# A 3x3 attention and convolution kernel: TensorE's loop over four image pairs is written out

## Chip, cores, metric

The kernel runs on one core of a Trainium2 chip. The metric is the device time of one launch in microseconds. TensorE (PE) does the matmuls, VectorE (DVE) and ScalarE (ACT) read its results from PSUM and prepare its next inputs, and SyncE (SP) issues nearly all DMAs. Each engine has its own program and its own loops; they meet only at semaphores.

## What is computed

```
x: [8,128,128,64] f32
q = x Q ; k, v = (3x3 neighbourhood of x) K, V
alpha = softmax over the 9 neighbours of (k . q) * mask
t_in = x + sum(alpha * v)
t = relu(conv3x3(t_in, ff1) + b1)      # 64 -> 64
t = relu(conv3x3(t,    ff2) + b2)      # 64 -> 128
t = relu(conv3x3(t,    ff3) + b3)      # 128 -> 64
out = t_in + t
```

## The kernel before

The eight images are worked as four pairs (`PAIRS`), two images side by side in the partitions. A pair is cut into 16 bands of 8 rows (`BANDS`) and takes 17 steps (`STEPS`, k = 0 to 16). A step runs the first and second convolution on one band, the third behind it, and the attention of the next band (at k = 16 that is the first band of the next pair); only step k = 15 (`BANDS - 1`) has no attention. The convolutions use a transformed form in which each row is split into four streams; the streams 2 and 1 are the "inner" ones and 0 and 3 the "outer" ones.

Every engine walks the same 17 steps for the four pairs. ACT, DVE and SP use `schedule` (L192 to L202): a hardware loop over the pairs (L193), in it steps 0 and 1, a hardware loop over steps 2 to 13 two at a time (L197), and steps 14, 15 and 16. TensorE has its own copy of this (L616 to L623): a hardware loop over the pairs (L616), steps 0 and 1, a hardware loop of 13 equal steps (L620), steps 15 and 16. Inside a hardware loop the counts to which a wait compares depend on the loop's registers, so each engine computes them with register instructions.

The order of work on TensorE at a step's start is what the prediction follows. `r_product(b)` (L372) makes the attention's first product in two PSUM banks, and `masks` (L388) presets the score banks. `conv1(..., outer=False)` (L445) does the inner streams of the first convolution. It may start when DVE has read the banks it overwrites (L871). With attention, it stops before the fourth of its first four weight sets (`await_r(b, 0)`, L464) until ACT has copied the result of `r_product` to SBUF (`keep_r`, L644, semaphore `r_ready`). Then come the rest of the inner streams, the scores of the first half (L396), and the outer streams (`outer=True`, also L445), for which DVE must have made the outer inputs (`t_inputs`, part 1, L799). The third convolution is L487, the second L503.

At a step's end `end2` (L503) does the last matmuls; its last two wait in `await_band` for DVE's additions (L781). In the last step of a pair (k = 16) DVE and ACT then still finish both halves of the second convolution (DVE L871, ACT L698, DVE L794 to L799) before they branch back to the top of their own pair loop.

Of the kernel before, what the change touches and what calls it, by code (L numbers as in the profile page):

```python
# [14 lines left out]
PAIRS = IMAGES // 2  # L15
# [59 lines left out]
def build(nc, x_bands, x_keys, qt2, kt, vbd, w1, w2, w3, b1, b2, b3, window, eye, eye16, out):  # L75
    with ExitStack() as ctx:
# [280 lines left out]
        def _(pe):  # L357
# [220 lines left out]
            def step(G, k, b, att):  # L578
                if att:
                    r_product(b)  # L580
                    masks()
                conv1(G, k, b, False, att)
                if att:
                    scores(b, 0)
                conv1(G, k, b, True)
                conv3_tile(G, k, 0)
                conv3_tile(G, k, 1, (lambda: await_prob(b, 0)) if att else None)
                if att:
                    turn(b, 0)
                conv3_tile(G, k, 2, (lambda: await_r(b, 1)) if att else None)  # L590
                if att:
                    masks()
                    scores(b, 1)
                conv3_tile(G, k, 3)
                if att:
                    mix(b, 0)
                begin2(G, k, 0)
                go_on2(G, k, 0)
                begin2(G, k, 1, (lambda: await_prob(b, 1)) if att else None)
                if att:  # L600
                    turn(b, 1)
                go_on2(G, k, 1)
                end2(G, k, 0)
                end2(G, k, 1)
                if att:
                    mix(b, 1)
                begin2(G, k, 2, (lambda: await_y(b)) if att else None)
                if att:
                    v_product(b)
                go_on2(G, k, 2)  # L610
                begin2(G, k, 3)
                go_on2(G, k, 3)
                end2(G, k, 2)
                end2(G, k, 3, lambda: await_band(b + 1 if att else b))

            with pe.Fori(0, PAIRS) as p:  # L616
                g0, b0 = p * STEPS, p * BANDS
                step(g0, 0, b0 + 1, True)
                step(g0 + 1, 1, b0 + 2, True)
                with pe.Fori(0, BANDS - 3) as h:  # L620
                    step(g0 + h + 2, 2, b0 + h + 3, True)
                step(g0 + (BANDS - 1), BANDS - 1, b0 + BANDS, False)
                step(g0 + BANDS, BANDS, b0 + BANDS, True)  # L623
# [433 lines left out]
```

## Time and profile before

| | us |
|---|---|
| median of 3 runs | 2279.57 (2278.01 to 2281.26) |
| the profiled execution | 2280.64 |
| its span, first to last instruction | 2278.5 |
| PE busy | 2183.9 (96%) |
| DVE busy | 1888.2 (83%) |
| ACT busy | 1132.8 (50%) |
| mean granted TensorE clock | 0.994 |

The profiled execution is 2.1 us longer than its span and 1.07 us above the median. In the views, times are us from the span's start. `PE` is a matmul and `PEld` a weight load; names that end in q (`PEldq`, `ACTq`, `DVEq`) are register and branch instructions of that engine's sequencer, which the busy time leaves out. The pairs begin on TensorE at about 49, 603, 1158 and 1713 us.

### The profile page before, as it was taken

How to read it: one execution, taken by the hardware profiler on the slowest of the kernel's cores; microseconds unless marked ns; L12 is line 12 of the kernel's file. 1: busy time of each engine (PE TensorE's matmuls, PEld its weight loads, DVE VectorE, ACT ScalarE, POOL GpSimd, SP SyncE). 2: the span in 40 equal slices, each digit the busy share in tenths (PEclk: the TensorE clock that was granted, in tenths of full speed). 3: DMA queues.
4: the chain of work that ended last, by engine and by line, in shares of the span. 5: the costliest groups of instructions: out<-in, count | busy, mean ns of one | idle time of the engine just before them, and what ended most of it. 6: DMA issues, size and time to landing. Idle time of an engine off the chain costs nothing.

```text
span 2278.5 us, 63905 instructions
## 1 busy us (share of the span) xinstructions
PE 2183.9 (96%) x24401; PEld 1226.9 (54%) x24401; DVE 1888.2 (83%) x2850; ACT 1132.8 (50%) x3108; POOL 15.5 (1%) x24
## 2 busy tenths in 40 slices
PE   4999999999899999999989999999988999999998
PEld 2655555555455555555455555555545555555554
DVE  4788888888688888888768888888877888888886
ACT  2555555544454554555345554555435555555543
POOL 2000000000000000000000000000000000000000
PEclk9999999999999999999999999999999999999999
DMA  5445544544355445544345455445434554454453
GB/s 131 137 138 154 157 146 133 166 151 135 98 164 160 147 132 163 153 145 132 128 139 154 132 168 148 144 137 168 145 122 116 169 146 142 142 167 144 139 152 124
DMA packets 291271, 328.54 MB, mean 144 GB/s; under 512 B 89300, under 2 KB 223252, under 8 KB 284564
## 3 DMA queue, kind: packets, MB, share of 16 engines
q1 hardware_dynamic: 291164, 327.17, 48.1%
q8 instruction: 60, 0.98, 0.2%
q14 instruction: 47, 0.39, 0.1%
HBM read 152.50 MB, written 33.82 MB: 82 GB/s over the span
## 4 chain that ended last, share of the span: by engine, by line
PE 86%; DVE 7%; issue 3%; ACT 2%; DMA 1%; SPq 1%; DVEq 0%; ACTq 0%
PE conv_banks L487 30%; PE conv_banks L503 24%; PE conv_banks L445 16%; PE mix_bank L423 5%; PE score_banks L396 4%; DVE work L871 3%; PE score_banks L408 3%; PE mix_bank L435 3%; PE score_banks L388 1%; DMA work<-w 1%; ACT probt L649 1%; DVE prob L770 0%; DVE negmax L761 0%; ACT relued L698 0%; PE mix_bank L372 0%
## 5 line engine op out<-in xcount | busy, mean ns | idle before, releaser
L487 PE MATMUL conv_banks<-dodd,w3f 128*64 128x512 f32 (+1 forms) x1656 | 500.8, 579 | 12.6 <-DVE work L838 9.8
L487 PE MATMUL conv_banks<-deven,w3f 128*64 128x512 f32 (+1 forms) x1656 | 494.7, 568 | 8.7 <-DVE prob L770 7.0
L632 ACT ACTIVATE prob<-score_banks,negmax 128x100 f32<-128x100 f32 x1040 | 343.0, 343 | 194.9 <-DVE negmax L761 194.9
L445 PE MATMUL conv_banks<-dt,w1f 128*64 128x256 f32 (+3 forms) x4224 | 413.4, 383 | 12.2 <-DVE work L871 5.6
L503 PE MATMUL conv_banks<-duh,w2h 64*128 64x512 f32 (+2 forms) x1632 | 327.7, 399 | 4.0 <-ACT m_sb L668 2.1
L445 PEld LDWEIGHTS conv_banks<-dt,w1f 128*64 128x64 f32 (+1 forms) x4224 | 219.0, 135 | 207.2 <-issue 71.2
L503 PE MATMUL conv_banks<-duh,w2l 64*128 64x512 f32 (+2 forms) x1632 | 318.7, 387 | 6.0 <-DVE prob L770 5.2
L503 PE MATMUL conv_banks<-dul,w2h 64*128 64x512 f32 (+2 forms) x1632 | 282.0, 396 | 0.9 <-DVE tf L781 0.9
L487 PEld LDWEIGHTS conv_banks<-dodd,w3f 128*64 128x64 f32 x1656 | 138.9, 137 | 237.6 <-issue 212.8
L649 ACT COPY probt<-score_banks 100x1024 f32<-100x1024 f32 x130 | 131.7, 1013 | 234.8 <-PE score_banks L408 234.8
L487 PEld LDWEIGHTS conv_banks<-deven,w3f 128*64 128x64 f32 x1656 | 155.8, 138 | 155.2 <-issue 111.5
L644 ACT COPY rq<-mix_bank 128x512 f32<-128x512 f32 x65 | 38.2, 587 | 387.2 <-PE mix_bank L372 387.2
L761 DVE TENSOR_REDUCE negmax<-score_banks 128x4 f32<-128x400 f32 x260 | 148.3, 571 | 98.5 <-PE score_banks L396 97.9
L632 ACT ACTIVATION_READ_ACCUMULATOR prob<-score_banks,negmax 128x1 f32 x1040 | 212.1, 204 | 0.0
L698 ACT ACTIVATE relued<-work,bias 128x1024 f32<-128x1024 f32 (+2 forms) x136 | 149.4, 1102 | 92.2 <-DVE work L871 92.2
L871 DVE TENSOR_TENSOR work<-conv_banks,work 128x1024 f32<-128x1024 f32 (+2 forms) x136 | 157.1, 1160 | 43.6 <-PE conv_banks L503 43.6
L503 PEld LDWEIGHTS conv_banks<-dul,w2h 64*128 64x128 f32 x1632 | 143.1, 185 | 75.5 <-issue 53.4
L503 PEld LDWEIGHTS conv_banks<-duh,w2l 64*128 64x128 f32 x1632 | 153.6, 185 | 49.4 <-ACT rq L639 15.2
L503 PEld LDWEIGHTS conv_banks<-duh,w2h 64*128 64x128 f32 x1632 | 153.2, 184 | 47.2 <-ACT m_sb L668 3.9
L668 ACT COPY m_sb<-conv_banks 128x512 f32<-128x512 f32 (+3 forms) x205 | 108.2, 562 | 137.0 <-PE conv_banks L487 98.5
L423 PEld LDWEIGHTS mix_bank<-probt,xk 100*64 100x64 f32 x4160 | 139.4, 139 | 58.0 <-issue 56.8
L811 DVE TENSOR_TENSOR dul<-work,duh 128x1024 fp32r<-128x1024 f32 (+1 forms) x136 | 159.0, 1169 | 0.0
(93 smaller groups left out, 2942.1 us busy)
## 6 DMA issues: line engine op xcount, KB each, us to landing
xk<-x_keys SPq DMA_DIRECT2D x66, 800.0 KB
xc<-x_bands SPq DMA_DIRECT2D x66, 650.0 KB, 5.0
dodd<-dodd SPq DMA_DIRECT2D x68, 512.0 KB, 5.1
xr<-x_bands SPq DMA_DIRECT2D x264, 128.0 KB, 3.4
out<-work SPq DMA_DIRECT2D x60, 512.0 KB, 2.7
dt<-dt SPq DMA_DIRECT2D x68, 256.0 KB, 2.3
deven<-deven SPq DMA_DIRECT2D x68, 256.0 KB, 5.6
duh<-duh SPq DMA_DIRECT2D x68, 256.0 KB, 2.4
```

The costliest lines, as they stand in the source:

```text
L396: mm = nc.tensor.matmul(banks[n][to, a], rq[rows, patch], xc[rows, :, patch * PATCH:patch * PATCH + HALO], start=False, stop=a == GROUP - 1)
L423: last = nc.tensor.matmul(mix_bank[image, a * C:(a + 1) * C], xk[:, patch, image], probt[:, half, i if a < GROUP else 1 - i, a], start=Tru ...
L445: mm = nc.tensor.matmul(bank[(LOWER, UPPER)[o], n * 256 + lo * 64:n * 256 + hi * 64], w1f[i][rows, m, s, o * C:o * C + C], dt[rows, lo + s ...
L487: return nc.tensor.matmul(bank[rows, lo * 128:hi * 128], w3f[:, m, s, odd * C:odd * C + C], source[:, lo + s // 2:hi + s // 2, m], start=s ...
L503: return nc.tensor.matmul(conv_banks[:, bank_of(which, j), lo * 128:hi * 128], w[rows, STREAMS[j], 2 * (which == EVEN) + s], d[rows, lo + ...
L632: last = nc.scalar.activation(prob[:, g % 2, a], score_banks[:, g % 2, a * KEYS:(a + 1) * KEYS], ACT.Exp, bias=negmax[:, g % 2, a:a + 1], ...
L649: nc.scalar.copy(probt[:, half], score_banks[0:KEYS].rearrange("n i (a q) -> n i a q", q=C)).then_inc(probt_ready, 1)
L668: nc.scalar.copy(m2_sb[:, which % 2, lo:hi], bank[:, lo:hi]).then_inc(act_read, 1)
L698: nc.scalar.activation(to[:, lo:hi, :, 1:1 + W], sums[which][:, lo:hi], ACT.Relu, bias=bias[:, 1:2]).then_inc(relu_done, 1)
L761: nc.vector.tensor_reduce(negmax[:, g % 2], score_banks[:, g % 2, 0:GROUP * KEYS].rearrange("q (a n) -> q a n", n=KEYS), AX_X, ALU.max, ne ...
L811: nc.vector.tensor_tensor(dul[:, 1:n + 1, streams], du[:, 0:n, streams], duh[:, 1:n + 1, streams].bitcast(F32), ALU.subtract).then_inc(du_ ...
L871: nc.vector.tensor_tensor(both, m03, both, ALU.add).then_inc(dve_read, 1)
```

## The change

TensorE's loop over the pairs becomes a loop of the program that builds the kernel, so the four bodies stand one behind the other in TensorE's program. `p`, `g0` and `b0` are then numbers. The loop over the 13 equal steps inside it stays a hardware loop, four times. The other engines are as before, with their loops over the pairs.

```
@@ -613,7 +613,7 @@
                 end2(G, k, 2)
                 end2(G, k, 3, lambda: await_band(b + 1 if att else b))
 
-            with pe.Fori(0, PAIRS) as p:
+            for p in range(PAIRS):
                 g0, b0 = p * STEPS, p * BANDS
                 step(g0, 0, b0 + 1, True)
                 step(g0 + 1, 1, b0 + 2, True)
```

## Rows read from the trace of the kernel before

**Rows 1.** The page, chain that ended last: shares of the span by engine
```profile
PE 86%; DVE 7%; issue 3%; ACT 2%; DMA 1%; SPq 1%; DVEq 0%; ACTq 0%
```

**Rows 2.** Who waited for whom, TensorE: us in total, times, longest
```profile
PE mix_bank L372 <- issue: 11.2, 3, 3.8
```

**Rows 3.** Line 616, TensorE's pair loop: ns min/median/max, first and last start
```profile
L616 PEldq COMPARE_BRANCH  x4: 83/3764/3870, 599.1 to 2263.9; - x4
```

**Rows 4.** Line 620, TensorE's inner loop, same columns
```profile
L620 PEldq COMPARE_BRANCH  x52: 76/215/247, 146.0 to 2205.9; - x52
```

**Rows 5.** Chain in order of time, an inner step: start us, us, what
```profile
1029.95 1.24 DVE work L871
...
1031.23 2.97 PE conv_banks L445 x32
```

**Rows 6.** Timeline around the first pair boundary: start, us, instruction, [idle before <- releaser]
```profile
599.01 0.33 PE L503 MATMUL conv_banks<-dul,w2h 64*128 64x128 f32 x2 [0.23 <-DVE tf L781]
...
600.12 0.74 DVE L871 TENSOR_TENSOR work<-conv_banks,work 128x256 f32<-128x256 f32 x2
...
601.28 0.51 ACT L698 ACTIVATE relued<-work,bias 128x256 f32<-128x256 f32 x1
...
602.97 1.12 PE L372 MATMUL mix_bank<-xc,qk 64*64 64x512 f32 x2 [3.64 <-issue]
...
604.99 0.58 ACT L644 COPY rq<-mix_bank 128x512 f32<-128x512 f32 x1 [3.21 <-PE mix_bank L372]
605.08 1.23 DVE L799 TENSOR_TENSOR dt<-tf 128x1024 f32<-128x1024 f32 x1 [1.77 <-issue]
...
605.22 6.00 PE L445 MATMUL conv_banks<-dt,w1f 128*64 128x256 f32 x31
...
612.01 5.54 PE L445 MATMUL conv_banks<-dt,w1f 128*64 128x256 f32 x32
```

**Rows 7.** Chain in order of time, the same boundary: conv1's two pieces
```profile
605.29 1.80 PE conv_banks L445 x12
...
607.20 3.96 PE conv_banks L445 x19
```

**Rows 8.** Line 193 at the three boundaries: ACT's branch, then its next instruction
```profile
L193 ACTq COMPARE_BRANCH  x1: 50/50/50, 601.0 to 601.0; - x1
L193 ACTq FUSED_REGOPS  x1: 73/73/73, 603.8 to 603.8; - x1
...
L193 ACTq FUSED_REGOPS  x1: 73/73/73, 1159.6 to 1159.6; - x1
...
L193 ACTq FUSED_REGOPS  x1: 73/73/73, 1714.4 to 1714.4; - x1
```

**Rows 9.** Timeline of TensorE at the second and third boundary
```profile
1167.67 0.65 PE L445 MATMUL conv_banks<-dt,w1f 128*64 128x256 f32 x4
...
1714.85 7.27 PE L445 MATMUL conv_banks<-dt,w1f 128*64 128x256 f32 x31
...
1722.90 1.30 PE L445 MATMUL conv_banks<-dt,w1f 128*64 128x256 f32 x10
```

**Rows 10.** Windows: stretch, its us, busy us (instructions) by engine, granted clock, DMA
```profile
602.57:605.98 3.41, 3.01 (x16) 1.08 (x18) 1.64 (x3) 0.99 (x2) 0.00 (x0) 0.50 0.70 178
...
1131.63:1135.05 3.42, 3.42 (x10) 1.00 (x8) 3.39 (x5) 1.31 (x8) 0.00 (x0) 0.50 0.02 5
...
1155.53:1162.35 6.82, 3.88 (x20) 1.56 (x22) 4.03 (x10) 2.29 (x5) 0.00 (x0) 0.50 0.60 141
...
1711.90:1718.72 6.82, 6.12 (x30) 2.73 (x30) 2.08 (x3) 1.07 (x2) 0.00 (x0) 0.50 0.65 174
```

**Rows 11.** Who waited for whom, TensorE, another wait of 2.2 us
```profile
PE conv_banks L487 <- DVE work L838: 9.8, 8, 2.2
```

**Rows 12.** Line 538, register instructions of TensorE: ns min/median/max
```profile
L538 PEldq ALU_OP  x204: 32/32/32, 75.7 to 2261.9; - x102
```

**Rows 13.** The page, DMA queues: packets, MB, share of 16 engines
```profile
q8 instruction: 60, 0.98, 0.2%
```

More of the change, by code:

```diff
@@ L614, in step @@
                 end2(G, k, 3, lambda: await_band(b + 1 if att else b))
-            with pe.Fori(0, PAIRS) as p:
+            for p in range(PAIRS):
                 g0, b0 = p * STEPS, p * BANDS
```

## The prediction

> **What bounds the kernel now.** I read the chain that ended last first: TensorE holds 86% of it [rows 1], so time comes off only where TensorE's own timeline gets shorter. Then I read who waited for whom. Among TensorE's waits stands one with the releaser "issue", that is, no semaphore: three times before L372, 11.2 us in total, 3.8 the longest [rows 2]. L372 is the first matmul of a step, and three is the number of returns to the top of the pair loop. The view of line 616 confirms it: the branch takes 3.70 to 3.87 us when taken (the minimum, 83 ns, is the last one, which falls through) [rows 3]. The branch of the inner loop takes 215 ns [rows 4], and in the inner step that I looked at it costs nothing: the convolution after it starts when DVE's L871 ends, and TensorE is then busy to the end of the step [rows 5]. So the change touches three stretches of some 10 us. The question for each is what is late next once the branch is gone.
>
> **What happens at a boundary.** In the first one, TensorE's last matmul ends at 599.01 + 0.33 = 599.34, the branch holds it until 602.97, and the second half of conv1 (the outer streams) begins at 612.01 [rows 6]. ACT and DVE keep their pair loops. ACT's branch starts at 601.0, its last work of the pair (L698) ends at 601.8, and its next instruction, a register operation, appears at 603.8 only, though it waits for nobody [rows 6, 8]. So ACT too pays about 2.8 us for going back. Today nobody sees that: the copy (L644) starts at 604.99, released by TensorE's L372, because TensorE was later still. DVE pays it as well: it is idle for 1.77 us before L799, with "issue" as the releaser [rows 6].
>
> **Part 1, the branch removed.** Without it TensorE goes on at 599.34. Product and masks take 1.49 us (1029.74 to 1031.23 in an inner step, whose end is in [rows 5]), so conv1 could start at 600.8. The banks are free by then: the first of DVE's two L871 ends near 600.5 [rows 6]. TensorE runs 12 matmuls of conv1, 1.8 us at most [rows 7], and stands at about 602.4 before the wait for `r_ready`. Behind that wait everything of TensorE is queued. ACT gives it: its register operation at 603.8, 0.1 to the copy (as DVE's next instruction at 605.0 is followed by L799 at 605.08), 0.58 for the copy [rows 6, 8], so TensorE goes on at about 604.6. Before, the same point was passed at 607.20 [rows 7]. That is 2.6 us won, not 3.6.
>
> From this point to the outer half it is 612.01 - 607.20 = 4.81 us at the full clock. I take these off the starts of the outer half at the other boundaries, 1167.67 and 1722.90 [rows 9], and get 1162.9 and 1718.1. ACT's register operation at 1159.6 and 1714.4 [rows 8] plus 0.8 gives 1160.4 and 1715.2. So 2.5 and 2.9 us are won. The sum is 8.0 us. DVE is not next: its L799 ends at 605.08 + 1.23 = 606.3 [rows 6], and the outer half is reached at 604.6 + 4.8 = 609.4. SP has its next transfer of the step behind the end of conv1, and all that it loaded for this step was waited for before the boundary.
>
> **Part 2, register work removed.** In the 16 steps outside the inner loops the counts of the waits become numbers. One such operation takes 32 ns [rows 12], and there are about 24 in a step, so the upper bound is 16 x 24 x 0.032 = 12 us. The sequencer runs them while the array still has matmuls queued. They show only behind a wait that ended late, and most of what ends late there is followed by the matmul itself. I take 0.5 us, near the lower end, as the rows around L372 show no idle but the branch's; a loss is excluded, since nothing is added to these steps. In the inner steps the additions stay: 0. The loop's own two register operations go with the branch.
>
> **Part 3, the clock.** Today the granted clock falls to half (1.2 instead of 2.4 GHz) at each boundary, for 3.4, 6.8 and 6.8 us [rows 10]. What this costs can be read off L445: in the first boundary the clock was low for the first 0.8 us of its 31 matmuls, in the third for 3.9 us, and they took 6.00 and 7.27 us [rows 6, 9]. That is 1.27 / 3.1 = 0.4 us lost per us at half clock. The working above is made from full-clock durations behind the wait, so a fall that remains has to be added. TensorE's idle time at a boundary is now 604.6 - 602.4 = 2.2 us in the first, and by the same working 2.6 and 3.3 in the others (restart less 3.1 us behind the last matmul). Such an idle of 2.2 us stands in the trace, before L487, once in each pair [rows 11]: the clock fell behind one of the three that I looked at, and was half for 3.4 us [rows 10]. Behind the three idles of 3.6 to 3.8 us it fell each time. The new ones lie between. I take 8.6 us at half clock in sum (today some 13 us with work in them), 8.6 x 0.4 = 3.5 us. The bounds are 0 and three times 6.8 us, that is 0 to 8.2 us.
>
> **Part 4, code.** The four bodies are longer than one, and all of it is fetched once. Today 60 packets of 16 KB are fetched on the instruction queue in 2278 us [rows 13], which is nothing beside the data, and it cannot rise much: every pair fetches its body anew already. That straight code is fetched ahead in time is seen in the outer steps of today's pairs, where the view of [rows 2] has no other wait of TensorE's matmuls for "issue": 0 us.
> The Trainium skill (Runtime: NRT & Kernel Launch, Instruction fetch mechanics) says that straight code is fetched ahead, that a taken branch to a place not held stalls, and that kernels prefer to be unrolled for that. By this alone the change would give all of the 11.2 us and the clock with it; the rows of ACT above speak against that, as the rule holds for ACT as well, which keeps its loop. The same section also says that only two blocks of 256 instructions are held. By that the inner loop (368 matmuls and as many weight loads) would stall in every turn; the 215 ns disagree.
>
> **Sum.** 2280.64 - 8.0 - 0.5 + 3.5 = 2275.6 us. Against the median of the runs, 2279.57, that is 4.0 us or 0.17% less. About 0.2% (4.6 us) is what a measurement of this kernel can tell from no change, so the forecast is within that, on the fast side.
>
> **Rivals.**
> *ACT is no obstacle.* It would be so if ACT's late return came from TensorE's (its fetch queued behind TensorE's). Against it: ACT's own branch starts 1.9 us after TensorE's and returns 0.9 us after it [rows 6, 8]. Then TensorE reaches the outer half at 599.34 + 1.5 + 1.5 + 4.8 = 607.1, 4.9 us earlier, and by the same working 5.2 and 6.3 at the others: 2280.64 - 16.4 - 0.5 = 2263.7 us.
> *The clock stays full* through the shorter idles: 2280.64 - 8.5 = 2272.1 us. For it speak the two idles of 2.2 us without a fall.
> *Nothing is won,* because the reload stays (the code behind the last step is not there in time after all), or because the clock takes all back: about 2280 us.
> *Slower: the inner branch stops being cheap.* It is cheap as long as the loop's code is still held when TensorE returns. In the new program the four inner loops lie at other places of the code, and if in one pair the body no longer fits what is held, each of its 12 returns costs what the pair's return costs today, 3.6 us, all of it seen: 43 us per pair, 2319 us or more. It decides from the first such loop. Against it: today's loop begins somewhere inside a block and still hits in all 48 returns [rows 4].
>
> **How the numbers follow.** The forecast (ACT's return is what TensorE waits for, part of the clock is lost) has a chance of 0.73 and spans 2273.5 to 2278.5; ACT no obstacle 0.06; full clock 0.10; nothing won 0.07; slower 0.04. The range of 8 in 10 reaches from just under the full-clock case to the nothing-won case: 2271.5 to 2280.0. Faster by over 0.2% is under 2275.0: a third of the forecast (0.24), full clock and no obstacle, 0.40. Slower is 0.04, the rest, 0.56, is within 0.2%.
>
> **What would show it.** Right: the wait before L372 for "issue" is gone; in its place stands an idle of 2 to 3.5 us before the thirteenth matmul of L445, released by ACT's L644, three times; ACT's idle before L644 no longer ends with PE. The inner steps keep 32.9 us. The granted clock tells how much of part 3 remained. Wrong: an idle of 3.7 us before L372 or an "issue" wait elsewhere on TensorE (part 4), inner branches of microseconds, or no wait for ACT at all.

## The result

The changed kernel takes 2285.38 us (median of 13 runs, 2282.30 to 2291.29), the kernel before on the same chips 2281.26 (13 runs, 2278.01 to 2283.05). The ratio is 1.0019, with a 95% interval of 1.0012 to 1.0027: 0.19% slower. The profiled execution took 2289.52 us with a span of 2287.5. Forecast were 2275.6 us and a range up to 2280.0. In a second set of runs, of both kernels beside each other again, the ratio was 1.0005 (0.9994 to 1.0016), with runs of the changed kernel from 2275.7 to 2287.1. So it is slower by 0.05 to 0.2%, the second interval takes in no difference at all, and neither takes in the 0.17% faster of the forecast.

The profile after, first who waited for whom on TensorE (us in total, times, longest):

```profile
PE conv_banks L445 <- ACT rq L644: 11.3, 3, 4.5
```

The row of before, L372 waiting for "issue" [rows 2], is gone. A wait of the same 11 us in sum stands in its place, three times, with ACT's copy as the releaser. The timeline of TensorE at the first boundary (start, us, instruction, idle before it and what ended it), to be held against [rows 6, 7]:

```profile
600.86 0.33 PE L503 MATMUL conv_banks<-dul,w2h 64*128 64x128 f32 x2
601.11 0.71 PE L372 MATMUL mix_bank<-xc,qk 64*64 64x512 f32 x2
...
602.70 1.51 PE L445 MATMUL conv_banks<-dt,w1f 128*64 128x256 f32 x12 [0.22 <-DVE work L871]
607.89 7.25 PE L445 MATMUL conv_banks<-dt,w1f 128*64 128x256 f32 x19 [3.67 <-ACT rq L644]
...
616.72 6.08 PE L445 MATMUL conv_banks<-dt,w1f 128*64 128x256 f32 x32
```

TensorE goes from L503 to L372 without a pause, waits 0.2 us for the banks of conv1, does the 12 matmuls, and then stands for 3.67 us. The 19 matmuls behind it took 3.96 us before [rows 7] and take 7.25 now. The same rows at the second and third boundary:

```profile
1165.20 7.24 PE L445 MATMUL conv_banks<-dt,w1f 128*64 128x256 f32 x19 [4.51 <-ACT rq L644]
...
1722.82 6.45 PE L445 MATMUL conv_banks<-dt,w1f 128*64 128x256 f32 x19 [3.07 <-ACT rq L644]
```

ACT's branch and the instruction behind it (line 193, durations in ns, start in us), which answer to [rows 8]:

```profile
L193 ACTq COMPARE_BRANCH  x1: 50/50/50, 603.0 to 603.0; - x1
L193 ACTq FUSED_REGOPS  x1: 73/73/73, 607.1 to 607.1; - x1
...
L193 ACTq COMPARE_BRANCH  x1: 45/45/45, 1159.5 to 1159.5; - x1
L193 ACTq FUSED_REGOPS  x1: 73/73/73, 1164.5 to 1164.5; - x1
...
L193 ACTq COMPARE_BRANCH  x1: 45/45/45, 1718.5 to 1718.5; - x1
L193 ACTq FUSED_REGOPS  x1: 73/73/73, 1722.1 to 1722.1; - x1
```

ACT's return took 4.1, 5.0 and 3.6 us here. And the windows with the clock at half (stretch, its us, busy us and instructions by engine, granted clock, DMA), which answer to [rows 10]:

```profile
607.60:617.84 10.24, 9.95 (x58) 5.08 (x60) 2.18 (x3) 1.68 (x6) 0.00 (x0) 0.50 0.18 62
1163.98:1174.22 10.24, 9.02 (x54) 4.52 (x56) 1.27 (x2) 1.66 (x3) 0.00 (x0) 0.50 0.22 63
1723.76:1730.59 6.83, 6.83 (x47) 3.50 (x46) 1.23 (x1) 0.59 (x1) 0.00 (x0) 0.50 0.14 51
```

27.3 us in sum at 1.2 instead of 2.4 GHz, 25.8 of them with TensorE at work. Before it was 17.1 us in sum, 13.0 of them with work [rows 10]. From the first L372 of step 16 to the first of step 1, before took 67.1, 69.0 and 68.5 us at the three boundaries and after takes 70.2, 70.6 and 69.9. The 6.1 us between the sums are most of the difference of the two profiles; another 2.2 us lie ahead of the first pair, where the start's transfers came later (step 0 of the first pair begins at 51.36 instead of 49.12). The change doesn't touch the start, and this moment lies between 48.8 and 52.2 us over all the profiles. The inner steps take 32.9 us as before.

### The profile page after: what moved, and what is told of

Read it like the earlier page. It is cut to its first block, busy times and chain, and to the rows that moved or that the text cites. A ratio compares the mean times of both kernels' runs of the same rounds, so it can differ in the third digit from the quotient of the medians.

```text
span 2287.5 us, 63569 instructions
## 1 busy us (share of the span) xinstructions
PE 2190.5 (96%) x24401; PEld 1232.0 (54%) x24401; DVE 1889.1 (83%) x2850; ACT 1132.9 (50%) x3108; POOL 15.5 (1%) x24
## 4 chain that ended last, share of the span: by engine, by line
PE 88%; DVE 6%; issue 3%; ACT 2%; DMA 1%; SPq 1%; DVEq 0%; ACTq 0%
PE conv_banks L487 29%; PE conv_banks L503 25%; PE conv_banks L445 18%; PE mix_bank L423 5%; PE score_banks L396 4%; DVE work L871 3%; PE score_banks L408 3%; PE mix_bank L435 3%; PE score_banks L388 1%; DMA work<-w 1%; ACT probt L649 1%; DVE prob L770 0%; ACT prob L632 0%; ACT relued L698 0%; DVE negmax L761 0%
## 5 line engine op out<-in xcount | busy, mean ns | idle before, releaser
L445 PE MATMUL conv_banks<-dt,w1f 128*64 128x256 f32 (+3 forms) x4224 | 420.0, 384 | 25.0 <-ACT rq L644 11.3
L445 PEld LDWEIGHTS conv_banks<-dt,w1f 128*64 128x64 f32 (+1 forms) x4224 | 221.9, 135 | 221.8 <-issue 84.9
L503 PE MATMUL conv_banks<-duh,w2h 64*128 64x512 f32 (+2 forms) x1632 | 328.4, 400 | 4.0 <-ACT m_sb L668 2.1
L503 PE MATMUL conv_banks<-duh,w2l 64*128 64x512 f32 (+2 forms) x1632 | 319.1, 388 | 6.0 <-DVE prob L770 5.2
L503 PE MATMUL conv_banks<-dul,w2h 64*128 64x512 f32 (+2 forms) x1632 | 281.9, 395 | 0.2
L649 ACT COPY probt<-score_banks 100x1024 f32<-100x1024 f32 x130 | 131.7, 1013 | 235.4 <-PE score_banks L408 235.4
L503 PEld LDWEIGHTS conv_banks<-dul,w2h 64*128 64x128 f32 x1632 | 143.3, 185 | 74.7 <-issue 51.9
L503 PEld LDWEIGHTS conv_banks<-duh,w2l 64*128 64x128 f32 x1632 | 153.7, 185 | 49.3 <-ACT rq L639 15.1
L503 PEld LDWEIGHTS conv_banks<-duh,w2h 64*128 64x128 f32 x1632 | 153.4, 184 | 47.2 <-ACT m_sb L668 3.9
```

Source lines behind the costliest of these rows:

```text
L445: mm = nc.tensor.matmul(bank[(LOWER, UPPER)[o], n * 256 + lo * 64:n * 256 + hi * 64], w1f[i][rows, m, s, o * C:o * C + C], dt[rows, lo + s ...
L503: return nc.tensor.matmul(conv_banks[:, bank_of(which, j), lo * 128:hi * 128], w[rows, STREAMS[j], 2 * (which == EVEN) + s], d[rows, lo + ...
L649: nc.scalar.copy(probt[:, half], score_banks[0:KEYS].rearrange("n i (a q) -> n i a q", q=C)).then_inc(probt_ready, 1)
```

## The experiments

Theory: TensorE waits for ACT because ACT comes back late from its own branch, and the clock that falls in this wait costs as much as the wait. Rivals: the straight code costs something itself; one bad draw; nothing but the wait.

**The changed kernel again.**

> The changed kernel once more, to have a second profile of it beside the next three on one chip. My theory: TensorE waits for ACT's L644 at each of the three later boundaries, because ACT reloads its own code after its branch; that took 3.6 to 5.0 us in the first profile of this kernel (2.9 to 4.0 in that of before), and behind the wait the clock is half for 6.8 to 10.2 us. Then the same wait (3 to 5 us, three times) stands here again, some step 0 of a pair lasts 38 to 42 us instead of 34.3, and the ratio to before is 1.001 to 1.003. Rival: the long reload and the long stretch at half clock were one bad draw; then ACT's reload is about 3.4 us on average here, and the ratio is 1.000 or less.

Ratio 1.0005 (0.9994 to 1.0016), median 2284.39 of 12 runs. The profiled run took 2276.98 us and is thus one of the fastest of the 12. Its timeline (the views end at 610, 1165 and 1718 us, so they count 14 and 16 of the 19 matmuls):

```profile
606.29 3.90 PE L445 MATMUL conv_banks<-dt,w1f 128*64 128x256 f32 x14 [2.67 <-ACT rq L644]
...
1161.94 3.31 PE L445 MATMUL conv_banks<-dt,w1f 128*64 128x256 f32 x16 [2.80 <-ACT rq L644]
...
1714.87 3.31 PE L445 MATMUL conv_banks<-dt,w1f 128*64 128x256 f32 x16 [2.30 <-ACT rq L644]
```

The wait stands in all three places but is shorter than I expected, and in step 0 the clock fell at the first only, for 6.8 us. (It also fell for 3.4 us in step 16 of the two later boundaries, behind the wait before conv3 that before has too [rows 11].) Step 0 took 39.0, 36.0 and 35.5 us. So the wait is lasting and its length is not: one and the same kernel gives 2277 or 2290 us. The ratio was below what I expected, and ACT's return took 3.1 us on average here, as the rival had it: the long draw is part of the first result, the wait itself is not a draw.

**ACT's pair loop written out too.**

```
 def schedule(eng, step, flat=False):
     ...
     if flat:
         for p in range(PAIRS):
             pair(p)
     else:
         with eng.Fori(0, PAIRS) as p:
             pair(p)
 ...
-            schedule(act, step)
+            schedule(act, step, flat=True)
```

> TensorE's and ACT's pair loops are both written out; DVE and SP keep theirs. My theory (ACT's reload is what TensorE waits for): the wait for L644 goes, TensorE goes through the boundary until the outer half of conv1, where DVE's own reload (L799 ready some 8 to 9.5 us behind TensorE's old branch, TensorE there at 7.8) may hold it by up to 1.5 us; the clock stays full at most boundaries. 4 to 5 us less than before at each of three boundaries: 2266 to 2270, ratio 0.994 to 0.995. Rival (the straight code of TensorE costs something itself, or the boundary is held by something else behind ACT): no faster than the changed kernel, 2283 to 2287.

2266.43 us, ratio 0.9930 (0.9917 to 0.9943). No wait for ACT's copy is left at the boundaries. What is next is what was expected, DVE's own return, at one boundary of three (the line numbers of this kernel are 4 higher, so L449 is conv1 and L803 DVE's outer inputs; the view ends inside the 32 matmuls):

```profile
609.74 2.57 PE L449 MATMUL conv_banks<-dt,w1f 128*64 128x256 f32 x19 [0.88 <-DVE dt L803]
```

Steps 16 and 0 together take 63.1, 63.9 and 62.2 us. Two loops written out give 18 us over one (2284.39 beside it): the straight code of TensorE is innocent, and ACT's branch is the cause of the wait.

**All four pair loops written out** (`flat=True` for ACT, DVE and SP).

> All four engines' pair loops are written out. My theory: as the run before, and DVE's reload goes too: no idle of TensorE at a boundary beyond 0.5 us, step 0 of a pair 33.3 us, full clock: 2263 to 2267, ratio 0.992 to 0.994. Rival (nothing but ACT matters): the same as the run before within 0.5 us. Rival (straight code costs): 2283 or more.

2264.90 us, ratio 0.9924 (0.9911 to 0.9937). Step 0 takes 33.1 us three times, and TensorE has no idle above 0.15 us in its first 14 us. The medians of this and the last kernel differ by 1.5 us, and their intervals overlap. The expected time was met; the expected full clock was not quite, it fell once in each pair for 3.4 us, in step 16 behind the wait before conv3 that before has too [rows 11].

**ACT's pair loop alone**, in the kernel before.

> The kernel before, TensorE's pair loop kept, ACT's pair loop written out. My theory: in the kernel before ACT's reload lies behind TensorE's own, so taking it away alone gives nothing: within 0.1% of before, and TensorE's 3.6 to 3.9 us before L372 stay. Rival (the reloads delay each other, being fetched by the same queues): TensorE's branch takes 0.3 us or more less, and the kernel is 1 to 3 us faster.

2281.42 us, ratio 0.9996 (0.9987 to 1.0005). TensorE's wait, with L376 for L372:

```profile
PE mix_bank L376 <- issue: 11.1, 3, 3.7
```

The same as in [rows 2], so one return doesn't lengthen the other to speak of. Written out alone, neither loop gains anything (1.0019 and 0.9996). Together they gain 0.7%.

**Work instead of idle time.** The real product is preceded by three that write the same values to the same banks:

```
 def step(G, k, b, att):
+    if k == 0 and G != 0:
+        for _ in range(3):
+            r_product(b, False)      # the same matmuls, without the semaphore
     if att:
         r_product(b)
```

> The changed kernel, with three more executions of the first attention product (L372, the same operands into the same banks, about 3.6 us of matmuls) ahead of the real one in step 0 of pairs 1 to 3. ACT could not have copied the result earlier, so the wait for ACT ends at the same time, but TensorE is busy for most of it. My theory (half of the loss is the clock that falls behind the wait): the idle before L445's thirteenth matmul shrinks from 3.4 to 4.5 us to 0 to 1.5, the clock stays full, and the kernel becomes 5 to 9 us faster than the changed one, 2276 to 2281, for all that it does more work. Rival (the wait alone is the loss): no gain, or 1 to 3 us slower than the changed kernel where the filler ends later than ACT's reload.

2275.59 us, ratio 0.9972 (0.9961 to 0.9983). The useless matmuls took 2.9 us at each boundary, not the 3.6 that I had expected: conv1 begins 4.28 us behind the first L372, TensorE busy throughout, where the changed kernel has 1.37 us of work. With them the kernel is 9 us faster than the changed one beside it (2284.39). Who waited on TensorE (L447 is conv1, L649 the copy):

```profile
PE conv_banks L447 <- ACT rq L649: 2.3, 2, 1.5
```

Two waits of 1.5 and 0.8 us are left, ACT's return took 2.7 to 4.7 us here, and in step 0 the clock stayed full at all three boundaries. In step 16 it fell for 3.4 us each time, ahead of the useless matmuls. The theory gave 2276 to 2281; the kernel is a little faster still.

**Waits of chosen length.** ACT and TensorE written out, and one ACT copy of chosen size ahead of the real one. The sizes n were 5, 9 and 13 in one kernel and 11, 16 and 21 in the other:

```
+    if k == 0 and G != 0:
+        to = spare[G // STEPS - 1]           # [128, n, 256]
+        nc.scalar.copy(to[:], zeros[:]...broadcast_to(to.shape))
     if att:
         keep_r(b, 0)
```

> TensorE's and ACT's pair loops written out, so that no reload delays ACT's copy L644, and one useless ACT copy of a chosen length ahead of it in step 0 of pairs 1, 2 and 3, which makes TensorE wait at its thirteenth matmul of L445 for about 1.1, 2.0 and 2.9 us. If the loss is wait plus clock: step 0 lasts 33.2 us plus the wait where the clock stays full, and 3 to 5 us more where it falls. My theory: it stays full at 1.1 and 2.0 and may fall at 2.9. Rival (the length of the wait doesn't matter to the clock, only the chance of the moment): falls at the short waits too.

> The same with useless copies that make the waits about 2.4, 3.4 and 4.5 us. My theory: the clock falls behind at least the two longer ones, and stays at half for 6.8 to 10.2 us, as in the first profile of the changed kernel, though nothing reloads here; step 0 then lasts 33.2 plus the wait plus 3 to 5 us. Rival (the long stretch at half clock comes with ACT's reload, not with the wait): the clock stays full or is half for 3.4 us only.

TensorE's timeline, of the first kernel (L450 is conv1, L649 the real copy):

```profile
604.50 4.08 PE L450 MATMUL conv_banks<-dt,w1f 128*64 128x256 f32 x19 [1.27 <-ACT rq L649]
...
1154.65 4.08 PE L450 MATMUL conv_banks<-dt,w1f 128*64 128x256 f32 x19 [2.12 <-ACT rq L649]
...
1708.15 5.96 PE L450 MATMUL conv_banks<-dt,w1f 128*64 128x256 f32 x19 [2.98 <-ACT rq L649]
```

and of the second:

```profile
607.22 6.05 PE L450 MATMUL conv_banks<-dt,w1f 128*64 128x256 f32 x19 [2.55 <-ACT rq L649]
...
1161.99 7.24 PE L450 MATMUL conv_banks<-dt,w1f 128*64 128x256 f32 x19 [3.61 <-ACT rq L649]
...
1721.66 7.24 PE L450 MATMUL conv_banks<-dt,w1f 128*64 128x256 f32 x19 [4.68 <-ACT rq L649]
```

The same 19 matmuls take 4.08 us behind the two short waits, 6.0 behind the two middle ones and 7.24 behind the long ones, though nothing reloads code on ACT in these kernels. The windows at half clock in the second kernel:

```profile
608.70:615.50 6.80, 6.80 (x48) 3.59 (x50) 1.15 (x2) 0.59 (x1) 0.00 (x0) 0.50 0.23 82
1161.60:1171.80 10.20, 9.81 (x58) 4.94 (x60) 2.05 (x3) 1.63 (x4) 0.00 (x0) 0.50 0.18 57
1721.40:1731.60 10.20, 9.94 (x58) 5.08 (x60) 1.71 (x3) 1.64 (x6) 0.00 (x0) 0.50 0.04 14
```

They last 6.8 and 10.2 us as in the changed kernel. The two kernels ran once each, in 2274.90 and 2290.41 us. This is the cleanest of the experiments: the wait alone makes the long stretches at half clock.

**The changed kernel a third time.**

> The changed kernel a third time, for a third profile: from the waits set by hand I expect step 0 to last 33.2 us plus the wait for L644 where that is up to 2.2 us, 3 us more where it is 2.5 to 3, and 4.5 us more where it is 3.6 or more. Rival: no such relation.

2287.85 us, one run. With it the table of the waits in these five profiles, in order of length (step 0 from its first L372 to that of step 1):

| wait, us | kernel | step 0, us | at half clock, us | step 0 - wait - 33.2 |
|---|---|---|---|---|
| 1.27 | hand-set | 34.5 | 0 | 0.0 |
| 2.12 | hand-set | 35.3 | 0 | 0.0 |
| 2.30 | changed, again | 35.5 | 0 | 0.0 |
| 2.55 | hand-set | 38.8 | 6.8 | 3.1 |
| 2.67 | changed, again | 39.0 | 6.8 | 3.1 |
| 2.71 | changed, third | 39.0 | 6.8 | 3.1 |
| 2.80 | changed, again | 36.0 | 0 | 0.0 |
| 2.98 | hand-set | 39.2 | 6.8 | 3.1 |
| 3.02 | changed, third | 40.9 | 10.2 | 4.7 |
| 3.07 | changed | 39.4 | 6.8 | 3.1 |
| 3.61 | hand-set | 41.3 | 10.2 | 4.5 |
| 3.67 | changed | 41.4 | 10.2 | 4.5 |
| 3.71 | changed, third | 41.6 | 10.2 | 4.7 |
| 4.51 | changed | 41.8 | 10.2 | 4.1 |
| 4.68 | hand-set | 42.4 | 10.2 | 4.5 |

33.2 us is step 0 without wait and at full clock (33.1 with all loops written out). Step 0 is 33.2 plus the wait, plus 0.45 us per us at half clock. The relation that I had written down holds in two of the three waits of this run; the one of 3.02 us, just outside the lengths that I had named, cost 4.7 instead of 3, and the one of 2.80 in the table cost nothing. So the length of the wait alone doesn't settle how long the clock stays at half.

**Both kinds of boundary in one execution.**

```
-            for p in range(PAIRS):
...
+            with pe.Fori(0, PAIRS // 2) as p2:
+                for half in range(2):
...
```

> TensorE's loop runs twice over two pairs that are written out, so the first and the third boundary are straight and the second returns to the loop's top, in one execution. By my theory the straight ones show the wait for ACT at L445 and the looped one the 3.7 us before L372 with no wait for ACT; steps 16 and 0 together last 67 to 69 us at the looped one and 66 (clock full) or 69 to 71 (clock fallen) at the straight ones, and the time lies between before and after, 2281 to 2286. Rival (the four written-out bodies cost by their length, not at the boundaries): the straight boundaries are no different from the looped one.

2288.58 us, ratio 1.0026 (1.0015 to 1.0036), above the expected range. The waits (L645 is the copy):

```profile
PE conv_banks L445 <- ACT rq L645: 7.3, 2, 3.7
...
PE mix_bank L372 <- issue: 4.6, 1, 4.6
```

As the theory has it: two straight boundaries with the wait for ACT, one looped one with the branch. The straight ones waited 3.75 and 3.59 us, with 10.2 and 6.8 us at half clock behind, and their steps 16 and 0 together take 70.4 and 70.3 us. At the looped one they take 69.5. Of that, 0.8 us come from the branch, which held L372 for 4.6 us, longer than any of [rows 2], and 1.7 from the clock, which also fell for 3.4 us in step 16; such a fall stands in one boundary of before too [rows 10]. Whether the long branch comes from the target's other place in the code or from chance was not tried, nor why the time isn't between before and after, as expected.

**The kernel before again.**

> The kernel before once more, for a second profile: does ACT's reload take as long here (3.4 us on average in the first) as with TensorE's loop written out (3.7 us over twelve boundaries, 2.8 to 5.0)? If TensorE's own reload shortens ACT's, the three here lie below 3.4 again; if the length is chance, they spread over 2.8 to 5.0 as well. Steps 16 and 0 together last 67 to 69 us.

2281.35 us, one run; steps 16 and 0 together take 67.2, 68.4 and 67.3 us. ACT's branch and what follows it, first and third boundary:

```profile
L193 ACTq COMPARE_BRANCH  x1: 50/50/50, 603.7 to 603.7; - x1
L193 ACTq FUSED_REGOPS  x1: 73/73/73, 607.7 to 607.7; - x1
...
L193 ACTq COMPARE_BRANCH  x1: 45/45/45, 1713.0 to 1713.0; - x1
L193 ACTq FUSED_REGOPS  x1: 73/73/73, 1718.7 to 1718.7; - x1
```

ACT's return takes 4.0, 2.9 and 5.7 us here: the length is chance, and no shorter with TensorE's loop in place (3.8 us on average over the six of the two profiles of before, 3.6 over the nine of the changed kernel). And the 5.7 us cost nothing: step 0 took 34.3 us. TensorE comes to the wait 607.20 - 602.97 = 4.2 us behind its L372 [rows 6, 7], 8.1 us behind its own branch, and covered even this one.

**The wait moved.** TensorE's wait for the copy goes from the middle of conv1's inner half to its end, in step 0 only:

```
-                        if att and n == 1 and i == 1:
+                        if att and k and n == 1 and i == 1:
                             await_r(b, 0)
...
                 if att:
+                    if k == 0:
+                        await_r(b, 0)
                     scores(b, 0)
```

> The changed kernel, with one wait moved: in step 0 of a pair TensorE waits for ACT's L644 not in the middle of conv1's inner half but behind it, just ahead of the scores, which are the first to need the copy. ACT's reload stays. My theory: TensorE does the 20 matmuls behind the old wait (about 4.8 us at the full clock) while ACT reloads; it comes to the wait some 7.9 us behind the first L372, and ACT's copy ends 5.4 to 7.6 us behind it, so the wait is 0 to 0.5 us; DVE's L799 may take its place with up to 1.5 us. The clock stays full: 2264 to 2269, ratio 0.993 to 0.995, nearly what writing out ACT's loop gave. Rival (it is not where the wait stands but that TensorE runs ahead of ACT and DVE at all): as the changed kernel, 2283 to 2286.

2266.23 us, ratio 0.9926 (0.9912 to 0.9939), with ACT's loop and its return as they are. The next wait is DVE's, as forecast (L801 is its outer inputs; the second view ends inside the 32 matmuls):

```profile
608.62 5.54 PE L445 MATMUL conv_banks<-dt,w1f 128*64 128x256 f32 x32 [0.31 <-DVE dt L801]
...
1159.02 4.14 PE L445 MATMUL conv_banks<-dt,w1f 128*64 128x256 f32 x26 [0.61 <-DVE dt L801]
```

Step 0 takes 33.3, 33.8 and 33.0 us. One wait moved over 20 matmuls turns a change that loses 0.2% into one that gains 0.7%.

**Both.** The moved wait and all four loops written out.

> All four pair loops written out and TensorE's wait for L644 moved behind conv1's inner half in step 0 as well. By my theory nothing is left to win by the second where ACT has no reload: the same as all loops written out alone, 2263 to 2266, ratio 0.992 to 0.993. Rival (the moved wait helps by itself): 2261 or less.

2263.23 us (2259.26 to 2264.41), ratio 0.9912 (0.9899 to 0.9926), the fastest kernel of the study. It was expected within 2263 to 2266 and is there, with a ratio just under the expected 0.992. Step 0 takes 32.77 us instead of 33.15 at each of the three boundaries, so the moved wait does give 0.4 us by itself, 1.1 in sum; the intervals of the two ratios overlap.

## Why the prediction was wrong

**Right.** That the returns to the loop's top, and nothing in the inner steps, were at stake; that ACT's late return takes their place at the thirteenth matmul of L445, three times; that DVE is not next but close behind (0.3 to 0.9 us once ACT is out of the way); that the straight code is fetched in time. The rule of the Trainium skill (Runtime: NRT & Kernel Launch, Instruction fetch mechanics) that straight code is fetched ahead and a branch to a place not held stalls holds in these traces, for TensorE's straight boundaries (no idle for "issue") and for ACT's branch (2.8 to 5.7 us) alike. The prediction set the 215 ns of [rows 4] against two blocks of 256 instructions; the same section of the Trainium skill also gives TensorE room for 2048, and with that the cheap return of the inner loop (some 740 matmuls and weight loads, 210 ns after the change) agrees. The banks of conv1, which the prediction had free, cost a wait of 0.2 us. Instruction packets fell from 60 [rows 13] to 54.

**Part 1, mis-sized.** The waits were forecast at 2.2, 2.6 and 3.3 us and measured 3.67, 4.51 and 3.07, 3.1 us more in sum. What failed here is the step that took ACT's register operations at 603.8, 1159.6 and 1714.4 [rows 8] as they were. They are three draws of a length that spreads from 2.8 to 5.7 us over the five profiles of the two kernels. Over the nine waits of the changed kernel the mean is 3.2 us, against 2.7 forecast. The sign for being right, an idle of 2 to 3.5 us, was passed at two of the three boundaries.

**Part 2, the size.** Less its branch, step 16 lasted 29.1 us (32.78 - 3.64) and lasts 28.8 now, where the clock is full; step 0 of the first pair lasts 34.15 instead of 34.44, and steps 14 and 15 together 61.1 instead of 61.2. Step 1 became 0.08 us longer in every pair, though a loss was called excluded. In sum some 1.2 us less, against 0.5 forecast; what of it is register work was not tried.

**Part 3, the term that decided.** This is the step of the prediction that failed most. I took 8.6 us at half clock in sum, with no working behind the number but that the new idles lie between the old ones. The three profiles of the changed kernel show 27.3, 6.8 and 27.3 us in step 0 of the later pairs. The price per us, 0.4, was nearly right (0.45). Wrong was the stretch: I had seen 3.4 us behind a wait of 2.2, and 3.4 to 6.8 behind 3.6 to 3.8 us, and put the new ones between. But behind the new wait stand other matmuls. Before, the half clock fell partly on idle time (of the 6.82 us at 1155.53 only 3.88 had a busy TensorE [rows 10]) and on L372. Now it begins about where the idle ends and lies on conv1 and the scores between its halves. It lasts 6.8 to 10.2 us, although TensorE is busy for nearly all of it. The idle's length is not the difference: behind the six idles of 3.6 to 3.9 us ahead of L372, in the two profiles of before, the clock was at half for 3.4 us once and for 6.8 five times; behind the five waits of 3.6 to 3.75 us in conv1 it was 10.2 four times and 6.8 once. That the kind of matmuls behind the wait keeps the clock down is my reading, and no run tries it: what TensorE did before the idle differs too. Shown is only that the wait alone brings the long stretch, and that the same place without wait stays at full clock.

The two terms explain the time: 2275.6 + 3.1 + (27.3 - 8.6) x 0.4 = 2286.2, and 2.2 us of late start give 2288.4 against the 2289.52 of the profile. The other way round, the profile with waits of 2.67, 2.80 and 2.30 us and 6.8 us at half clock took 2276.98, within 1.4 us of the forecast. (The sum starts from the profiled 2280.64 and saves 5.0 us; set against the median of 2279.57 it was written as 4.0.)

**The range and the rivals.** My upper bound for the clock, 8.2 us, was in the text (2280.3 us); it assumed no more than 6.8 us at each boundary, and the range ended at 2280.0. With 10.2 us and a wait of 4.5 us at each boundary the same working gives 2280.64 - 8.5 + 5.4 + 12.2 = 2289.7. The rival that ended on the slower side was the wrong one (the inner branches still take about 0.21 us). The right one was written into the forecast itself, with a size that couldn't turn its sign: an idle about as long as the old one, behind which the clock stays at half for twice as much work (25.8 us against 13.0).

## What to carry to other kernels

Where several engines return to a loop's top at the same place, each can pay microseconds for it (2.7 to 5.7 here), and they hide one another. Removing it on one engine shows the next; write out the loops of all that meet there, or put work between the return and the first wait for the engine that still returns. Before removing a stall on TensorE, ask not only how long the idle that is left will be but what stands behind it, since that work may run at half clock, and for longer than before. Take the length of a reload, or of any transfer, from as many occurrences as the profile has, and let the sum see the longest of them.

## What the runs showed of the hardware

Behind one and the same wait in front of the same matmuls, the clock stayed full for waits up to 2.30 us, and fell behind eleven of twelve from 2.55 to 3.75 us (not behind one of 2.80) and behind both above 4. Once down it stayed at half for 6.8 or 10.2 us with TensorE busy nearly throughout; before, it was 3.4 or 6.8. At 0.45 us lost per us, a wait of 3.7 us costs 8.2. 2.9 us of useless matmuls ahead of the wait, at each of three boundaries, made the kernel 9 us faster.

These lengths hold for this place only. Behind the wait of 2.1 to 2.2 us before conv3 in step 16, the clock fell for 3.4 us at 19 of the 42 boundaries of the 14 profiles, of before and after alike; step 16 of the changed kernel then lasts 30.5 us instead of 28.8.

The return to a loop's top took 2.7 to 5.7 us on ACT and 3.7 to 4.6 on TensorE where the body is long, and 0.2 us for TensorE's inner loop of some 740 matmuls and weight loads.
